# Layer 1 of a four-layer residual chain turned round: rows stationary, weights moving, activations transposed

## The chip, the core and the metric

The kernel runs on one core of a Trainium2 chip. The metric is the device time of one launch in microseconds (us). The engines are TensorE (PE; its weight loads are listed apart as PEld), VectorE (DVE), ScalarE (ACT), GpSimd (POOL) and SyncE (SP), each with a queue of its own that it works off in order. PSUM is where TensorE's results land; a bank holds 512 f32 per partition.

## What is computed

x has 64 batches of 32 rows of 512 values, 2048 rows in all. Four layers follow each other, each adding to x. Layer 1 is a gated MLP with three rank-16 adapters chosen per batch; it is what the change is about.

```python
def lora_add(base, inp, A, B):
    Ab = A[layer_idx][lora_indices]
    Bb = B[layer_idx][lora_indices]
    t = jnp.einsum('bri,bni->bnr', Ab, inp)
    return base + jnp.einsum('bor,bnr->bno', Bb, t) * SCALE        # SCALE 0.5, rank 16
gate = lora_add(jnp.einsum('bnh,fh->bnf', x, W_gate), x, A_gate, B_gate)   # h 512, f 1376
up = lora_add(jnp.einsum('bnh,fh->bnf', x, W_up), x, A_up, B_up)
act = jax.nn.silu(gate) * up
down = lora_add(jnp.einsum('bnf,hf->bnh', act, W_down), act, A_down, B_down)
...
x = x + _L0_cond_ref(x, ...)                       # layer 1, above
x = x + _L1_cond_ref(x, itok_B_0_15, ...)          # a 32x32 mix of the rows of each batch
x = x + _L2_cond_ref(x, itok_B_0_7, ...)           # 512x512 product, top-2 of 8 experts of rank 16
x = x + _L3_cond_ref(x, L3_cond_weights, itok_B_0_15)   # another 32x32 mix
```

All inputs are f32. Each f32 operand of a product is split into a high and a low part (type fp32r), and each product is three matmuls: high x high, high x low, low x high.

## The kernel before

**Layer 1, tiles.** The rows go in 8 groups (`g`) of 256, and F = 1376 in 11 chunks (`f`) of 128, the last of 96; a step `s` is one chunk of one group, 88 steps. In `gate_up_base` a chunk of W_gate or W_up is stationary (128 of H by 128 of F) and the transposed rows `xt` move, 256 columns: 2 weights x 4 pieces of H x 3 matmuls. So gate and up stand in PSUM with F on the partitions, which is what the down product needs as its stationary operand. `gate_up_adapters` adds the rank products: B of the chunk stationary, t moving, 2 x 3 matmuls of 256. `down` has 128 rows of the activations stationary and W_down moving: 2 row tiles x 2 halves of H x 3 matmuls of 288 columns, 256 of W_down and 32 of A_down beside them. `x_a` makes t = A x of the next group (24 matmuls of 256), and `transpose_td` and `down_adapters` finish the adapter of the down product, one step into the next group.

**Engines beside it.** ScalarE applies silu (L691) and makes every high part (L673, L677); VectorE multiplies by up (L867) and makes the low parts (L833, L891); GpSimd makes the low parts of W_down (L634) and issues the gathers of the adapters' tables (L572: `a`, `b`, `bd`). The order of all this is one list, `lane_jobs(s)`, that ScalarE, VectorE and (for W_down) GpSimd walk through alike; TensorE waits for `s_lo` with the number of a job in it. `plain_loads(s)` is the order of SyncE's loads, `gathers(s)` that of GpSimd's. PSUM holds three gate/up tiles, two down tiles and one for t and td.

**Weights.** W_gate, W_up and W_down are loaded and split once, during the first group, and stay in SBUF. SyncE's queue holds the loads back at two places: until the gathers of A have landed ("adapters first"), and until TensorE is within five chunks (`LOADS_AHEAD`).

**The end of layer 1.** In the last three steps the first tiles of layers 2 to 4 are mixed in (`l1`, `transpose_x2`, `l2_base`); the loop behind them takes 16 tiles of 128 rows through these layers.

## Time and profile before

| | us |
|---|---|
| median of 3 runs (lowest, highest) | 635.86 (635.08, 636.76) |
| the profiled execution | 636.53 |
| its span, first to last instruction | 634.6 |
| its mean granted TensorE clock | 0.992 |
| busy: PE, DVE, ACT, POOL | 604.6, 300.7, 202.4, 211.1 |
| layer 1, up to its last product | about 526 |

The profile is one execution. A matmul's duration is longer than its place in the stream, since matmuls are pipelined: what a matmul costs is read from the start times of its neighbours in the timeline. In the names, out<-in, buffer numbers are left out.

### The profile page before, as it was taken

What the parts mean: (1) busy time and instruction counts of PE and PEld (TensorE: products, weight loads), DVE (VectorE), ACT (ScalarE), POOL (GpSimd) and SP (SyncE); (2) the same over time, 40 slices, a digit from 0 to 9 for tenths busy, and PEclk for the clock granted to TensorE, in tenths of its full rate; (3) what the DMA queues carried; (4) which work ended last, traced back from release to release, by engine and by line L of the source; (5) the groups of instructions that cost most, each with busy time, mean ns of one, the idle gap of its engine ahead of it and who ended that gap; (6) DMA issues with size and microseconds to landing.
All of it is one profiled execution on the core that took longest, in us unless ns stands there. A gap on an engine that the chain in (4) does not pass through costs nothing.

```text
span 634.6 us, 11455 instructions
## 1 busy us (share of the span) xinstructions
PE 604.6 (95%) x4659; PEld 593.2 (93%) x4659; DVE 300.7 (47%) x748; ACT 202.4 (32%) x514; POOL 211.1 (33%) x230
## 2 busy tenths in 40 slices
PE   4797899999999999999999999999999998999996
PEld 4797899999999999999999999999999998888885
DVE  4575344234324332442333234333432257998997
ACT  4463332232223222322232223222323243333421
POOL 4347225111511241033113211420145714565541
PEclk9899799999999999999999999999999999999999
DMA  6875024102510241033104212411142112222212
GB/s 202 259 249 173 27 67 159 54 11 74 164 39 24 79 151 34 24 110 120 40 20 134 93 41 58 136 56 37 34 149 107 53 33 68 68 67 88 79 53 81
DMA packets 26612, 55.79 MB, mean 88 GB/s; under 512 B 4224, under 2 KB 7744, under 8 KB 26560
## 3 DMA queue, kind: packets, MB, share of 16 engines
q1 hardware_dynamic: 18608, 31.17, 15.0%
q0 software_dynamic: 7808, 23.86, 12.6%
q8 instruction: 36, 0.59, 0.4%
q14 instruction: 16, 0.13, 0.1%
q10 hardware_dynamic: 144, 0.03, 0.0%
HBM read 46.66 MB, written 8.39 MB: 87 GB/s over the span
## 4 chain that ended last, share of the span: by engine, by line
PE 83%; DVE 9%; issue 4%; DMA 1%; ACT 1%; POOL 1%; SPq 1%; POOLq 0%; DVEq 0%; ACTq 0%
PE gu_ps L1041 16%; PE gu_ps L1039 16%; PE gu_ps L1040 16%; PE down_ps L1039 8%; PE down_ps L1040 8%; PE down_ps L1041 8%; PE l_ps L1039 2%; PE l_ps L1041 2%; DVE route L940 2%; PE l_ps L1040 2%; DVE x L958 2%; DVE route L939 1%; PE tg_ps L1039 1%; PE tg_ps L1041 1%; PE tg_ps L1040 1%
## 5 line engine op out<-in xcount | busy, mean ns | idle before, releaser
L1039 PE MATMUL gu_ps<-xt,wgu_sb 128*128 128x256 f32 (+1 forms) x704 | 201.3, 286 | 8.3 <-DVE wgu_sb L891 8.3
L1041 PE MATMUL gu_ps<-xt,wgu_sb 128*128 128x256 f32 (+1 forms) x704 | 200.5, 285 | 0.4 <-issue 0.4
L1040 PE MATMUL gu_ps<-xt,wgu_sb 128*128 128x256 f32 (+1 forms) x704 | 200.5, 285 | 0.0
L1039 PEld LDWEIGHTS gu_ps<-xt,wgu_sb 128*128 128x128 f32 (+1 forms) x704 | 134.5, 191 | 8.4 <-DVE wgu_sb L891 8.3
L867 DVE TENSOR_TENSOR act<-act,gu_ps 128x256 f32<-128x256 f32 (+1 forms) x88 | 36.9, 420 | 217.9 <-ACT act L691 206.4
L1041 PEld LDWEIGHTS gu_ps<-xt,wgu_sb 128*128 128x128 f32 (+1 forms) x704 | 134.7, 191 | 0.7 <-issue 0.7
L1040 PEld LDWEIGHTS gu_ps<-xt,wgu_sb 128*128 128x128 f32 (+1 forms) x704 | 134.5, 191 | 0.0
L572 POOL DMA_INDIRECT b_sel_raw<-b_gu,idx_rank x48 | 46.4, 967 | 236.2 <-PE gu_ps L1041 222.3
L691 ACT ACTIVATE act<-gu_ps 128x256 f32<-128x256 f32 (+1 forms) x88 | 33.7, 383 | 261.4 <-PE gu_ps L1041 254.9
L1039 PE MATMUL down_ps<-wd_sb,act_hl 128*128 128x288 f32 (+1 forms) x352 | 104.9, 298 | 0.4 <-DVE act_hl L833 0.4
L1041 PE MATMUL down_ps<-wd_sb,act_hl 128*128 128x288 f32 (+1 forms) x352 | 104.0, 295 | 0.0
L1040 PE MATMUL down_ps<-wd_sb,act_hl 128*128 128x288 f32 (+1 forms) x352 | 103.9, 295 | 0.0
L572 POOL DMA_INDIRECT a_raw<-a_all,idx_batch x64 | 63.6, 993 | 69.9 <-DVE wd_sb L891 47.6
L1039 PEld LDWEIGHTS down_ps<-wd_sb,act_hl 128*128 128x128 f32 (+1 forms) x352 | 66.8, 190 | 0.7 <-DVE act_hl L833 0.7
L1040 PEld LDWEIGHTS down_ps<-wd_sb,act_hl 128*128 128x128 f32 (+1 forms) x352 | 66.6, 189 | 0.0
L1041 PEld LDWEIGHTS down_ps<-wd_sb,act_hl 128*128 128x128 f32 (+1 forms) x352 | 66.3, 188 | 0.0
L833 DVE TENSOR_TENSOR act_hl<-act,act_hl 128x256 fp32r<-128x256 f32 (+1 forms) x88 | 38.6, 439 | 38.3 <-ACT act_hl L673 33.1
L1039 PE MATMUL gu_ps<-t_hl,b_sel 128*128 128x256 f32 (+1 forms) x176 | 50.2, 285 | 1.8 <-DVE t_hl L833 1.8
L673 ACT CAST act_hl<-act 128x256 fp32r<-128x256 f32 (+1 forms) x88 | 35.8, 407 | 50.0 <-DVE act L867 45.8
L1041 PE MATMUL gu_ps<-t_hl,b_sel 128*128 128x256 f32 (+1 forms) x176 | 50.3, 286 | 0.0
L1040 PE MATMUL gu_ps<-t_hl,b_sel 128*128 128x256 f32 (+1 forms) x176 | 50.1, 285 | 0.0
L1039 PE MATMUL l_ps<-w2ra_hl,x2t_hl 128*128 128x328 f32 (+1 forms) x128 | 42.7, 334 | 0.6 <-DVE x_res L861 0.2
(132 smaller groups left out, 1017.8 us busy)
## 6 DMA issues: line engine op xcount, KB each, us to landing
wgu_sb_raw<-wgu SPq DMA_DIRECT2D x20, 256.0 KB, 5.7
xt_raw<-x_t SPq DMA_DIRECT2D x16, 256.0 KB, 3.1
x_res<-x_rows SPq DMA_DIRECT2D x8, 512.0 KB
x_after_l<-x_res SPq DMA_DIRECT2D x8, 512.0 KB
x<-x_after_l SPq DMA_DIRECT2D x16, 256.0 KB, 3.1
out<-y SPq DMA_DIRECT2D x15, 256.0 KB, 2.1
wd_sb_raw<-wd SPq DMA_DIRECT2D x10, 256.0 KB, 5.7
w_raw<-w2ra_t SPq DMA_DIRECT2D x1, 1296.0 KB
```

What stands on the lines that cost most here:

```text
L572: nc.gpsimd.indirect_dma_start(out=dst, out_offset=None, in_=table, in_offset=bass.IndirectOffsetOnAxis(ap=idx, axis=0)).then_inc(s, 16)
L673: sc.copy(out_, in_).then_inc(s_hi, 1)
L691: sc.activation(act[0:k, s % 2, :], gu_ps[s % GU_BANKS][0:k, 0, :], ACT.Silu).then_inc(s_silu, 1)
L833: ve.tensor_tensor(out_, raw, high.bitcast(F32), ALU.subtract).then_inc(s_lo, 1)
L867: ve.tensor_tensor(act[0:k, s % 2, :], act[0:k, s % 2, :], gu_ps[s % GU_BANKS][0:k, 1, :], ALU.mult).then_inc(s_mul, 1)
L939: link(ve.tensor_scalar(g1, const("iota"), ids[:, 1:2], w1, ALU.is_equal, ALU.mult))
L940: link(ve.tensor_tensor(g0, g0, g1, ALU.add))
L958: ve.tensor_tensor(halves(x3[:, t % 3, :], a, b), halves(x2[:, t % 3, :], a, b), base_of(t, a, b), ALU.add).then_inc(s_x3, 1)
L1039: pe.matmul(out_, stationary[0], moving[0], start=start, stop=False, skip_group_check=True)
L1040: pe.matmul(out_, stationary[0], moving[1], start=False, stop=False, skip_group_check=True)
L1041: return pe.matmul(out_, stationary[1], moving[0], start=False, stop=stop, skip_group_check=True)
```

## The change

- **Rows stationary.** The rows go in 16 tiles (`i`) of 128, F in three chunks (`n`) of 352, 512 and 512 columns, the narrow one first; 48 steps. `gate` and `up` have 128 rows of `xt` stationary and the weights moving, up to 512 columns. Each gate and each up has a PSUM bank of its own, two of each; down has one tile instead of two.
- **A x.** The columns of A (128) lie beside the narrow chunk's gate columns, so that t comes out of the same matmuls, 480 columns wide. Only the first tile has it apart (`x_a`).
- **Transposes.** The activations now have rows on the partitions. `transpose_act` turns the 128-column pieces of a chunk (3, 4 and 4) by a matmul against the identity; high and low part are made from its PSUM tile `act_t`. `transpose_t` turns t (2), `transpose_td` td (1).
- **Rank products stacked.** t is written twice side by side, so that its transpose holds it twice, in partitions 0 to 63 and 64 to 127: the upper copy as high part, the lower as low part. One matmul against B's high part does two of the three products, a second one on 64 rows the third (`stacked`). B is gathered doubled, 128 rows for four batches, for each tile of 128 rows.
- **Loads.** Weight pieces of a quarter chunk; SyncE's two hold-backs are gone. The loads of x, its stores and the residual go by tile.
- **Second stage.** The same instructions; layer 2's mix uses one PSUM tile, not four, and the hand-over at the end of layer 1 is ordered anew.

```diff
-GROUP = 256
-NG = ROWS // GROUP
...
+TR = TB * RANK
...
+CHUNKS = [(1024, F), (0, 512), (512, 1024)]
+NC = len(CHUNKS)
+STEPS = NT * NC
...
 def plain_loads(s):
...
-                + ["adapters first", ("wgu", GU_BANKS, 0), ("wgu", GU_BANKS, 1), ("wd", 0)]
...
+        return ([("x", 0, 0), first[0], first[1], ("x", 0, 1)] + first[2:] + wgu_items(0, 1)
+                + wgu_items(1, 0) + [("wd", f) for f in pieces_of(0)] + wgu_items(1, 1)
+                + wgu_items(2, 0) + [("wd", f) for f in pieces_of(1)] + wgu_items(2, 1)
+                + [("x", 1, 0)] + [("wd", f) for f in pieces_of(2)])
...
-        gu_ps = [ps(f"gu_ps{i}", [2, GROUP], banks_a) for i in range(GU_BANKS)]
-        down_ps = [ps(f"down_ps{i}", [2, H], banks_a) for i in range(TILES)]
-        tg_ps = ps("tg_ps", [2, GROUP], banks_a)
+        gu_ps = [[ps(f"gu_ps{i}_{m}", [H], banks_a) for m in range(2)] for i in range(2)]
+        down_ps = ps("down_ps", [2, H], banks_a)
+        act_t = ps("act_t", [HC, P], banks_a)
+        t_ps = ps("t_ps", [HC, P], banks_a)
...
+                elif kind == "act":
+                    s = job[1]
+                    sc.wait_ge(s_actt, s + 1)
                     if s >= 2:
                         sc.wait_ge(s_d, s - 1)
-                    hi(act_hl[0:k, s % 2, 0, :], act[0:k, s % 2, :])
+                    for k, j0, j1 in act_blocks(s):
+                        ins = sc.copy(act_hl[0:k, s % 2, 0, j0:j1, :], act_t[0:k, j0:j1, :])
+                    ins.then_inc(s_hi, 1)
...
+            def stacked(out_, stationary, moving):
+
+
+                pe.matmul(out_, stationary, moving[0], start=False, stop=False, skip_group_check=True)
+                return pe.matmul(out_, stationary[0:TR], moving[1][0:TR], start=False, stop=True,
+                                 skip_group_check=True)
...
+                    mm = product(out_, x_of(i, c), gate_moving(i, n, c), c == 0, False)
...
+                    product(up_of(s), x_of(i, c), wgu_parts(n, 1, c)[1:], c == 0, False)
...
+            def transpose_act(s):
+                pe.wait_ge(s_mul, s + 1)
+                if s >= 1:
+                    pe.wait_ge(s_lo, s_lo_of(("act", s - 1)))
+                for j, f in enumerate(pieces_of(s % NC)):
+                    w = cw(f)
+                    mm = pe.transpose(act_t[0:w, j, :], act[:, s % 2, j * P:j * P + w], ident)
+                mm.then_inc(s_actt, 1)
...
             for s in range(STEPS):
...
+                i, n = divmod(s, NC)
+                gate(s, 0, HC // 2)
+                if n == 1 and i >= 1:
+                    transpose_td(i - 1)
+                gate(s, HC // 2, HC)
+                if s >= 1:
+                    transpose_act(s - 1)
+                up(s, 0, HC // 2)
+                if n == 1 and i >= 1:
+                    down_adapters(i - 1)
+                if s == STEPS - 1:
+                    l1(0)
+                up(s, HC // 2, HC)
+                if n == 0:
+                    if i == 0:
+                        x_a(0)
+                    transpose_t(i)
+                else:
+                    adapters(s)
...
+                if s >= 1:
+                    down(s - 1)
...
+                if n == 0:
+                    adapters(s)
```

TensorE before, around the transposes of td (`tg_ps<-const_sb,td`) in the second chunk of a later group; `gu_ps` is the PSUM of gate and up, `xt` the rows, `wgu_sb` the weights:

```order
L1041 MATMUL gu_ps<-xt,wgu_sb 128x256
L1115 MATMUL tg_ps<-const_sb,td 128x128 [waits s_mask]
L1115 MATMUL tg_ps<-const_sb,td 128x128
L1039 MATMUL gu_ps<-xt,wgu_sb 128x256
L1040 MATMUL gu_ps<-xt,wgu_sb 128x256
...
L1039 MATMUL gu_ps<-t_hl,b_sel 128x256 [waits s_lo]
...
L1039 MATMUL down_ps<-wd_sb,act_hl 128x288 [waits s_mask,s_x1,s_lo]
```

TensorE after, in the narrow chunk of a later tile, from the last gate matmul to the rank products; `act_t` and `t_ps` are the PSUM tiles of the transposes, `wg_sb` and `wu_sb` the narrow chunk's weights:

```order
L1055 MATMUL gu_ps_0<-wg_sb,xt 128x480
L1120 MATMUL act_t<-const_sb,act 128x128 [waits s_lo,s_mul]
L1120 MATMUL act_t<-const_sb,act 128x128 x3
L1053 MATMUL gu_ps_1<-wu_sb,xt 128x352
...
L1100 MATMUL t_ps<-const_sb,t_m 128x128 [waits s_tm]
L1100 MATMUL t_ps<-const_sb,t_m 128x128
L1053 MATMUL down_ps<-wd_sb,act_hl 128x288 [waits s_lo]
...
L1060 MATMUL gu_ps_0<-b_sel,t_hl 128x352 [waits s_lo]
L1061 MATMUL gu_ps_0<-b_sel,t_hl 128x352
```

Stationary and moving operand have changed sides, the transposes stand between gate and up, and the down product behind them waits for the low part made from `act_t`.

ScalarE before, in the weight load of the first group, from A to the first silu (`agu_t` and `wd_sb<-a_raw` are A, `b_sel` is B):

```order
L677 CAST agu_t<-a_raw 128x512 [waits s_a_in]
L677 CAST agu_t_up<-a_raw 128x512 [waits s_a_in]
L677 CAST wd_sb<-a_raw 128x4x32 x4
L673 CAST b_sel<-b_sel_raw 128x512 [waits s_b_in0]
L673 CAST wgu_sb<-wgu_sb_raw 128x512 [waits s_wgu_in3_0]
L673 CAST t_hl<-t_raw 128x512 [waits s_mask]
L673 CAST b_sel<-b_sel_raw 128x512 [waits s_b_in1]
L673 CAST wgu_sb<-wgu_sb_raw 128x512 [waits s_wgu_in3_1]
L673 CAST wd_sb<-wd_sb_raw 128x2x256 [waits s_wd_in0]
L691 ACTIVATE act<-gu_ps 128x256 [waits s_gu]
```

ScalarE after, the same stretch of the first tile:

```order
L679 CAST wg_sb<-a_raw 128x4x128 [waits s_a_in]
L675 CAST b_sel<-b_sel_raw 128x704 [waits s_b_in0]
L675 CAST t_hl<-t_ps 128x256 [waits s_tt]
L675 CAST w_sb<-w_sb_raw 128x512 [waits s_wgu_in1_0_0]
L675 CAST w_sb<-w_sb_raw 128x512 [waits s_wgu_in1_0_1]
L675 CAST w_sb<-w_sb_raw 128x512 [waits s_wgu_in1_0_2]
L675 CAST w_sb<-w_sb_raw 128x512 [waits s_wgu_in1_0_3]
L691 ACTIVATE act<-gu_ps_0 128x352 [waits s_gu]
```

The high part of t now stands right behind B's, ahead of all wide weight pieces (`w_sb`); before, six weight pieces of 512 stood ahead of A, and two more between A and the first silu. VectorE's low parts follow in the same order.

## Rows read from the trace of the kernel before

**Rows 1.** The page, part 1: busy us of the engines, share of the span, instructions.

```profile
PE 604.6 (95%) x4659; PEld 593.2 (93%) x4659; DVE 300.7 (47%) x748; ACT 202.4 (32%) x514; POOL 211.1 (33%) x230
```

**Rows 2.** Busy time by stage: stretch and its length, engines' busy us, granted clock, DMA.

```profile
8.34:93.69 85.35, 74.86 (x552) 74.08 (x553) 47.71 (x92) 39.04 (x96) 37.68 (x35) 0.94 0.51 161
93.69:500.00 406.31, 406.31 (x3301) 406.31 (x3300) 145.14 (x341) 115.44 (x307) 110.02 (x115) 1.00 0.25 78
500.00:526.40 26.40, 25.65 (x192) 24.51 (x190) 12.89 (x31) 10.32 (x22) 8.26 (x12) 1.00 0.11 30
526.40:634.60 108.20, 97.78 (x619) 88.34 (x618) 93.00 (x283) 34.17 (x86) 52.99 (x65) 1.00 0.22 74
```

**Rows 3.** Timeline of PE in group 2: start us, us, engine, line, op.

```profile
199.90 0.28 PE L1039 MATMUL gu_ps<-xt,wgu_sb 128*128 128x256 f32 x1
...
201.94 0.28 PE L1041 MATMUL gu_ps<-t_hl,b_sel 128*128 128x256 f32 x1
202.06 0.30 PE L1039 MATMUL down_ps<-wd_sb,act_hl 128*128 128x288 f32 x1
...
203.65 0.28 PE L1039 MATMUL tg_ps<-xt,agu_t 128*128 128x256 f32 x1
```

**Rows 4.** Timeline of PE: td transposes of group 1, and those of group 2.

```profile
155.26 0.38 PE L1115 MATMUL tg_ps<-const_sb,td 128*128 128x128 f32 x2
155.40 0.36 PE L1039 MATMUL gu_ps<-xt,wgu_sb 128*128 128x256 f32 x1
155.60 0.28 PE L1040 MATMUL gu_ps<-xt,wgu_sb 128*128 128x256 f32 x1
...
216.83 0.38 PE L1115 MATMUL tg_ps<-const_sb,td 128*128 128x128 f32 x2
```

**Rows 5.** Timeline of PE in the second stage: widths of 328, 320 and 512, four transposes.

```profile
540.65 0.31 PE L1039 MATMUL l_ps<-w2ra_hl,x2t_hl 128*128 128x328 f32 x1
...
542.32 0.31 PE L1041 MATMUL l_ps<-w2ra_hl,x2t_hl 128*128 128x328 f32 x1
...
544.30 0.60 PE L1147 MATMUL x2t_ps<-const_sb,x 128*128 128x128 f32 x4
544.65 0.39 PE L1039 MATMUL l_ps<-w2ra_hl,x2t_hl 128*128 128x320 f32 x1
544.88 0.31 PE L1040 MATMUL l_ps<-w2ra_hl,x2t_hl 128*128 128x320 f32 x1
...
545.62 0.28 PE L1039 MATMUL l_ps<-b_hl,hgt_hl 128*128 128x256 f32 x1
...
546.32 0.39 PE L1039 MATMUL l_ps<-x_hl,bd_hl 128*128 128x512 f32 x1
...
547.72 0.31 PE L1039 MATMUL l_ps<-w2ra_hl,x2t_hl 128*128 128x328 f32 x1
```

**Rows 6.** Timeline: a transpose to PSUM, then its low part on DVE.

```profile
512.83 0.60 PE L1147 MATMUL x2t_ps<-const_sb,x 128*128 128x128 f32 x4
...
514.28 0.68 DVE L902 TENSOR_TENSOR x2t_hl<-x2t_ps,x2t_hl 128x512 fp32r<-128x512 f32 x1
```

**Rows 7.** Waits of PE before 93.6 us: us in total, times, longest.

```profile
PE gu_ps L1039 <- DVE wgu_sb L891: 8.3, 1, 8.3
PE tg_ps L1039 <- DVE agu_t L891: 6.6, 1, 6.6
PE gu_ps L1039 <- DVE t_hl L833: 1.8, 1, 1.8
```

**Rows 8.** Groups of instructions, shapes apart: busy us, mean ns, idle time before.

```profile
L891 DVE TENSOR_TENSOR wgu_sb<-wgu_sb_raw,wgu_sb 128x512 fp32r<-128x512 f32 x20 | 16.7, 861 | 4.4 <-ACT wgu_sb L673 4.4
...
L634 POOL TENSOR_TENSOR wd_sb<-wd_sb_raw,wd_sb 128x512 fp32r<-128x512 f32 x10 | 13.1, 1307 | 24.5 <-ACT wd_sb L673 24.4
...
L673 ACT CAST wgu_sb<-wgu_sb_raw 128x512 fp32r<-128x512 f32 x20 | 11.8, 617 | 2.3 <-DMA wgu_sb_raw<-wgu 2.0
```

**Rows 9.** Busy time in the densest stretch of the weight load.

```profile
32.00:40.00 8.00, 7.56 (x61) 7.32 (x60) 5.99 (x10) 5.01 (x11) 3.92 (x3) 1.00 0.96 318
```

More of the change, by code:

```diff
@@ L78, with cw, width, pieces_of @@
 L2_COLS = sum(L2_WIDTH)
-def w13_tiles(n):
-    return range(n * NT // W13_STEPS, (n + 1) * NT // W13_STEPS)
-def cw(c):
-    return P if c < FC - 1 else LASTW
+def cw(f):
+    return min(P, F - f * P)
+def width(n):
+    return CHUNKS[n][1] - CHUNKS[n][0]
+def pieces_of(n):
+    return range(CHUNKS[n][0] // P, -(-CHUNKS[n][1] // P))
+WD_ORDER = [f for n in range(NC) for f in pieces_of(n)]
 CONST_COLS = {}
@@ L146, in gathers @@
[L146 to L155 removed]
+    if s >= 1 and s + 1 < STEPS:
+        out.append(("b", s + 1))
+    if n < 2 and i + 1 < NT:
+        out += [("a", i + 1, b) for b in range(n * TB // 2, (n + 1) * TB // 2)]
+    if n == 2:
+        out.append(("bd", i))
+    if 0 <= s - W13_FIRST < NT:
+        out.append(("w13", s - W13_FIRST))
+    return out
@@ L626, in _ @@
             for s in range(-1, STEPS):
-                first = [it for it in gathers(s) if it[0] == "b" or s < 0]
+                first = [it for it in gathers(s) if s < 0 or it[0] == "b"]
                 for it in first:
@@ L894, in add_x2 @@
+                ins.then_inc(s_lo, 1)
             def add_x2(t):
@@ L1129, in mix, with down_adapters @@
+            def down_adapters(i):
+                pe.wait_ge(s_lo, max(s_lo_of(("td", i)), s_lo_of(("bd", i))))
+                for half in range(2):
+                    cols = slice(half * HALF, (half + 1) * HALF)
+                    mm = stacked(base_cols(i)[:, half, :], td_hl[:], [bd_hl[:, part, cols] for part in range(2)])
+                mm.then_inc(s_dl, 1)
             def mix(bank, t, m, x_hl):
@@ L1256, with act_blocks @@
 N_IDX = IDX_RANK + 3 + 2
-def first_step(k):
-    return k // PAIRS * FC + k % PAIRS * 2
-def mask_no(job):
-    order = [j for s in range(-1, STEPS + FC) for j in lane_jobs(s) if j[0] in ("t", "td")]
-    return order.index(job) + 1
+CHUNKS_AT = [sum(width(k) for k in range(n)) for n in range(NC)]
+def act_blocks(s):
+    ks = [cw(f) for f in pieces_of(s % NC)]
+    full = sum(k == P for k in ks)
+    return [(P, 0, full)] + [(k, full, full + 1) for k in ks[full:]]
 def kernel(**inputs):
```

871 lines of the change are left out of this document (408 added, 463 removed).

## The prediction, made before the changed kernel was run

> **What bounds the kernel now.** The page's first part gives TensorE 95% of the span [rows 1]; that share alone doesn't say that matmuls set the end, so the second view is the busy time by stage [rows 2]. There the reader sees four stretches. From 8.34 to 93.69 us the weights arrive and TensorE runs 552 matmuls in 85.35 us. From 93.69 to 500 us TensorE is busy for all of 406.31 us, at a granted clock of 1.00, while VectorE works 145 us and ScalarE 115 us. From 500 to 526.4 us the second stage's first tiles are mixed in. From 526.4 us on layers 2 to 4 run, 108.2 us, with VectorE busy 93.0. So layer 1 is bound by the column stream of TensorE and the tail mostly by VectorE. The third view is the timeline, for the price of a matmul: not its duration (0.28 us, pipelined), but the distance from start to start.
>
> **Prices, start to start.** 256 columns: from 199.90 to 201.94 are 17 steps, 0.120 us each; 288 columns: 12 steps from 202.06 to 203.65, 0.1325 us [rows 3]. 328 columns: 11 steps from 540.65 to 542.32, 0.1518; 320 columns: 5 steps from 544.88 to 545.62, 0.148; 512 columns: 6 steps from 546.32 to 547.72, 0.2333 [rows 5]. At full clock a column is 0.4167 ns, so the rest of one matmul is 13.3 ns at 256 columns and 20 ns at 512: wider is hardly cheaper by the column. 352 and 480 columns don't occur; a line between 328 and 512 gives 0.1624 and 0.2191. Four transposes in a row take 0.35 us and make the first matmul behind them 0.23 instead of 0.148, together 0.43 [rows 5]; two take 0.14 and 0.08 behind them, 0.22 [rows 4]. Three are then 0.36 and one is 0.16.
>
> **The change, layer 1 in the steady part.** A group of 256 rows takes 216.83 - 155.26 = 61.57 us [rows 4]. The sum gives the same: 366 matmuls of 256 columns (264 gate and up, 66 rank, 24 for A x, 12 of the last rank product) x 0.120 = 43.9, 132 of 288 x 0.1325 = 17.5, two transposes 0.2; 61.6. Of the changed kernel, one tile of 128 rows is:
> gate and up of the two wide chunks with their stacked rank products, 2 x (12 + 12 + 4) = 56 of 512 columns, 13.07 us;
> gate of the narrow chunk with A x attached, 12 of 480, 2.63;
> its up and rank products, 12 + 4 of 352, 2.60;
> down, unchanged, 66 of 288, 8.75;
> the last rank product, 4 of 256, 0.48;
> 11 transposes of the activations in blocks of 4, 4 and 3, two of t and one of td, 0.43 + 0.43 + 0.36 + 0.22 + 0.16 = 1.60.
> Together 29.13 us, 58.26 for 256 rows: 3.31 less than 61.57. Times 8 it is **26.5 us less**. What goes: a third of the rank products (the low part of t now sits in the idle 64 rows of the stationary), half of the columns of A x, and the 32 padded columns of F. What comes: 14 transposes per tile where there was one.
>
> **Does it still run without a wait?** Before, no wait of TensorE is found between 93.69 and 500 us [rows 2]. The new chain is: silu, product, transposes, high part, low part, then down. The tightest place is at the narrow chunk, where down of the last wide chunk follows the transposes after only 12 up matmuls and the transposes of t: 0.43 + 12 x 0.1624 + 0.22 = 2.6 us from the first transpose. What has to fit in: a chain of the same shape and size stands in the trace, four transposes starting at 512.83 and the low part ending at 514.28 + 0.68 = 514.96, so 2.13 us [rows 6], with VectorE's mask of t beside it and done before. Slack 0.5 us. The other chunks have 12 x 0.2333 + 4 x 0.2333 = 3.7 us for it. I take no wait, and keep 0.5 us per tile, 8 us, as the upper bound. VectorE has 145 busy in 406 us and ScalarE 115 [rows 2]; the wider operations carry the same elements, plus b gathered and split for each 128 rows instead of 256, some 2.5 us per tile and engine: room enough. The doubled gathers of b (11 MB more) lie beside 78 GB/s of traffic where 318 are reached [rows 2, 9], with a whole chunk, some 10 us, to land in.
>
> **The start.** Before: the 552 matmuls up to 93.69 us are 420 of 256 and 132 of 288 columns, 50.4 + 17.5 = 67.9 us of stream in 85.35, so 17.4 us are lost after the first matmul, besides the 8.3 in front. The waits show where: 6.6 for A of the next group, 1.8 for t [rows 7]; the rest is the lower clock (0.94 over the stretch [rows 2]) and short waits. After: the same weights must be in place within one tile, 29 us, not within 61. The first pieces are smaller (a quarter of a chunk, half of the rows), so the first matmul comes about 0.9 us earlier, at 7.4. The narrow chunk's 24 matmuls end near 13.5, a part of them at the low clock. Then A x, mask, transposes, high, low and the gathered rank weights stand in one row in front of the first rank product, with nothing for TensorE beside them: about 6 us, to 19.5. From there VectorE must split 16 wide weight pieces at 0.861 [rows 8], 13.8 us, two rank tables of twice the width (0.68 for 512 [rows 6], so 1.3 each), 2.6, and some 2.5 of activations; 19 us. ScalarE has 16 + 7 pieces x 0.617 [rows 8] plus 4.5, also 19, and the transfers, about 10 MB at 318 GB/s [rows 9], end near 35 us. So the last rank product of tile 0 ends near 39.5, with down of its last two chunks still to come. By stream alone that point would be 7.4 + 21.8 = 29.2. Lost: 10.3, and 1.7 more for the clock after the pause, 12; bounds 8 (pieces at 0.7) and 16 (a gather behind the now unthrottled weight queue). **Gain at the start: 17.4 - 12 + 0.9 = 6.3 us** (2 to 10).
>
> **The end of layer 1.** The pieces of the second stage that are mixed in are the same. One PSUM tile for layer 2 instead of four makes each product wait for the sum before it; I find these sums done in time, but the residual sum of the last tile now stands right in front of the next matmul, about 0.8 us. From there on nothing is changed: 108.2 us.
>
> **Sum.** -26.5 - 6.3 + 0.8 = -32.0 us. The profiled execution had a span of 634.6 and a time of 636.5, 0.7 over the median of 635.9; I carry the difference over to the median: 635.9 - 32.0 = **603.9 us**.
>
> **A rule of the Trainium skill against it.** The four transposes above are 128x128 in f32, and cost 0.43 us together. The Trainium skill, "TensorE: Matmul & The Clock Gate", Part 4, gives some 275 ns for one transpose within a kernel. By the page's price 14 of them would be 3.85 us per tile, 36 us more in all. The trace has that figure only as the duration of one, not as its place in the stream. [...]
>
> **Rivals.** (a) *Wide matmuls at the narrow overhead*: the 20 ns at 512 columns belong to those products, which read other tiles, and gate and up pay 13.3 as at 256. Then 56 x 6.6 ns + 28 x about 4 ns = 0.48 us per tile less, 7.7 in all: 596. For it: no gate product of that width is in the trace. Against: 320 and 328 columns already lie above the line of 256 and 288. (b) *A wait per chunk or tile*, the chain of transposes late at down: 0.5 to 1 us per tile, 8 to 16: 612 to 620. For it: 0.5 us of slack, and two engines in order with gathers in front. Against: the chain in the trace fits. (c) *Transposes that don't pipeline with their neighbours*, each at its full duration (0.38 for two [rows 4], so 0.27 for one): 14 x 0.27 = 3.8 instead of 1.6 per tile, +35 us, **639, slower**. It tips above 1.60 + 32 / 16 = 3.6 us of transposes per tile. Against: four in 0.35 [rows 5], in the same form. (d) *The start doesn't improve*, the weights being needed twice as fast: 610.
>
> **Chances.** Forecast (with the start anywhere in its bounds) 0.62, its own range 599 to 610; (a) 0.14; (b) 0.15; (c) 0.03; something else that adds a wait in each chunk 0.03; (d) counted beyond the bounds 0.03. Range 595 to 616: it takes in (a) and the lower half of (b). A difference below 0.3%, 1.9 us, can't be told from none. Faster by more 0.94, within 0.02, slower 0.04.
>
> **What would show it.** In the timeline after: 0.233 us from start to start in gate and up of 512 columns, 0.162 and 0.219 at 352 and 480; 0.43 per block of four transposes with the next matmul; a period of 29.1 us from one td transpose to the next; no wait of TensorE between the second and the fifteenth tile. The first td transpose shows the start. Wrong if the period is above 30, if TensorE waits at down's first matmul for the low part, or if its clock falls below 1.00 in the steady part.

## The result, and the profile after

| | us |
|---|---|
| before, median of 4 (lowest, highest) | 635.80 (635.08, 636.76) |
| forecast | 603.9 (595 to 616) |
| after, median of 4 (lowest, highest) | 658.89 (657.33, 662.34) |
| ratio after to before, 95% interval | 1.037 (1.032 to 1.042) |
| span of the profiled executions, before and after | 634.6 and 659.0 |

The change makes the kernel 3.7% slower, where 5% faster was forecast. The miss is 55 us. The page of after, part 1, against [rows 1]:

```profile
PE 626.0 (95%) x3359; PEld 517.3 (78%) x3359; DVE 324.0 (49%) x686; ACT 205.1 (31%) x413; POOL 234.8 (36%) x238
```

TensorE has 1300 instructions fewer and is busy 21 us longer. Its busy time by stage (stretch and length, busy us of PE, PEld, DVE, ACT and POOL, granted clock, DMA share, GB/s), against [rows 2]:

```profile
0.00:66.10 66.10, 48.34 (x211) 38.74 (x212) 38.54 (x64) 32.39 (x62) 36.76 (x32) 0.87 0.63 209
66.10:497.00 430.90, 430.90 (x2259) 349.43 (x2258) 165.19 (x296) 119.43 (x230) 130.58 (x124) 1.00 0.31 100
497.00:545.00 48.00, 47.47 (x269) 39.64 (x268) 23.85 (x44) 16.90 (x33) 14.16 (x17) 1.00 0.28 94
545.00:659.00 114.00, 99.27 (x626) 89.47 (x625) 96.44 (x283) 36.34 (x90) 53.34 (x65) 1.00 0.20 68
```

From 66.1 to 497 us TensorE is busy for all of 430.9 us at a granted clock of 1.00. So no wait and no clock explains the loss: the stream itself is longer than the sum said. Its period from one td transpose to the next, which is one tile of rows, follows from the first and the fifteenth of them in the timeline of PE, (513.81 - 66.25) / 14 = **31.97 us**; forecast 29.1:

```profile
66.25 0.27 PE L1144 MATMUL t_ps<-const_sb,td 128*128 128x128 f32 x1
...
513.81 0.27 PE L1144 MATMUL t_ps<-const_sb,td 128*128 128x128 f32 x1
```

Within the period the same timeline shows which distance is wrong. First the places with an answer as forecast: 480 columns, 352 columns and the transposes (start us, duration us, engine, line, operation; what counts is the distance of the starts):

```profile
278.84 0.38 PE L1053 MATMUL gu_ps<-wg_sb,xt 128*128 128x480 f32 x1
...
281.24 0.38 PE L1055 MATMUL gu_ps<-wg_sb,xt 128*128 128x480 f32 x1
281.46 0.60 PE L1120 MATMUL act_t<-const_sb,act 128*128 128x128 f32 x4
281.81 0.41 PE L1053 MATMUL gu_ps<-wu_sb,xt 128*128 128x352 f32 x1
282.06 0.33 PE L1054 MATMUL gu_ps<-wu_sb,xt 128*128 128x352 f32 x1
...
283.65 0.32 PE L1055 MATMUL gu_ps<-wu_sb,xt 128*128 128x352 f32 x1
```

480 columns take 2.40 / 11 = 0.218 us each, 352 take 1.59 / 10 = 0.159, and the block of four transposes 0.35 + 0.25 - 0.16 = 0.44. Then the rank products of a wide chunk:

```profile
305.72 0.39 PE L1055 MATMUL gu_ps<-w_sb,xt 128*128 128x512 f32 x1
305.95 0.39 PE L1060 MATMUL gu_ps<-b_sel,t_hl 128*128 128x512 f32 x1
306.26 0.50 PE L1061 MATMUL gu_ps<-b_sel,t_hl 64*128 64x512 f32 x1
306.69 0.49 PE L1060 MATMUL gu_ps<-b_sel,t_hl 128*128 128x512 f32 x1
307.12 0.50 PE L1061 MATMUL gu_ps<-b_sel,t_hl 64*128 64x512 f32 x1
307.55 0.40 PE L1053 MATMUL down_ps<-wd_sb,act_hl 128*128 128x288 f32 x1
307.78 0.30 PE L1054 MATMUL down_ps<-wd_sb,act_hl 128*128 128x288 f32 x1
```

Up to 305.95 the starts are 0.23 us apart (the first two lines, and those ahead of them). Then they are 0.31, 0.43, 0.43, 0.43 and 0.23 apart, and the last of these was to be 0.13. The only thing that sets L1061 apart is the form: its stationary has 64 rows, 64*128 in the place of 128*128. The weight loads of the same place tell how the distance arises; in brackets is the idle time ahead of a load and what it was put down to ("issue": nothing that the profile shows):

```profile
305.72 0.19 PEld L1060 LDWEIGHTS gu_ps<-b_sel,t_hl 128*128 128x128 f32 x1
306.26 0.18 PEld L1061 LDWEIGHTS gu_ps<-b_sel,t_hl 64*128 64x128 f32 x1 [0.35 <-issue]
306.69 0.19 PEld L1060 LDWEIGHTS gu_ps<-b_sel,t_hl 128*128 128x128 f32 x1 [0.24 <-issue]
307.12 0.18 PEld L1061 LDWEIGHTS gu_ps<-b_sel,t_hl 64*128 64x128 f32 x1 [0.24 <-issue]
307.55 0.19 PEld L1053 LDWEIGHTS down_ps<-wd_sb,act_hl 128*128 128x128 f32 x1 [0.25 <-issue]
307.65 0.19 PEld L1054 LDWEIGHTS down_ps<-wd_sb,act_hl 128*128 128x128 f32 x1
```

Normally a load starts with the matmul ahead of its own (the load of L1060 at 305.72, its matmul at 305.95). At each change between 128 and 64 rows, at 306.26, 306.69, 307.12 and 307.55, the load starts only with its own matmul, and the stream is longer by about the 0.19 us that a load takes. That these changes cost the time was the theory to be tested.

Two smaller differences are left, the start and the second stage. The start: the waits of PE before 90 us (us in total, times, longest), against [rows 7], and the granted clock between 16 and 30 us:

```profile
PE gu_ps L1053 <- DVE wg_sb L837: 11.1, 2, 6.5
PE t_ps L1100 <- DVE t_m L846: 3.5, 2, 2.0
...
```

```profile
16.00:22.00 6.00, 3.11 (x14) 2.92 (x14) 1.98 (x4) 1.34 (x2) 0.00 (x0) 0.50 1.04 373
22.00:30.00 8.00, 6.99 (x20) 4.54 (x19) 4.79 (x8) 6.60 (x14) 3.10 (x3) 0.60 1.07 372
```

Then the second stage, whose code is nearly the same: from the first to the last hgt transpose (the transpose of `hg`, layer 2's gated rank values, one per tile) it takes 97.7 us before (529.1 to 626.9) and 101.1 after (549.7 to 650.9). Its period per tile of rows is either 6.5 to 6.7 or 7.1 to 7.2 us, but for the last one of 3.5; before, 4 of 15 periods are long, after 9 of 15. In a short one VectorE (first three lines) and GpSimd (fourth) look so, in the timeline of before:

```profile
561.03 0.29 DVE L939 TENSOR_SCALAR route<-const_sb,route 128x8 f32<-128x8 f32 x1
561.35 1.14 DVE L940 TENSOR_TENSOR route<-route 128x8 f32<-128x8 f32 x1
562.53 0.29 DVE L944 TENSOR_TENSOR hg<-l_ps,route 128x128 f32<-128x128 f32 x1
...
561.12 1.34 POOL L623 TENSOR_TENSOR x_hl<-x,x_hl 128x512 fp32r<-128x512 f32 x1 [2.57 <-ACT x_hl L742]
```

In a long one, in the timeline of after (the same instructions stand 12 lines lower in the kernel, on GpSimd 11):

```profile
603.40 1.43 DVE L951 TENSOR_SCALAR route<-const_sb,route 128x8 f32<-128x8 f32 x1
604.86 0.65 DVE L952 TENSOR_TENSOR route<-route 128x8 f32<-128x8 f32 x1
605.54 0.29 DVE L956 TENSOR_TENSOR hg<-l_ps,route 128x128 f32<-128x128 f32 x1
...
603.50 1.30 POOL L634 TENSOR_TENSOR x_hl<-x,x_hl 128x512 fp32r<-128x512 f32 x1 [2.58 <-ACT x_hl L743]
```

A routing operation on 8 values takes 0.16 to 0.29 us when undisturbed, and 1.14 or 1.43 when GpSimd's subtraction of 512 columns runs at the same time. In the first case one operation is held, in the second two in a row: from the start of L939 to that of L944 1.50 us pass, from L951 to L956 2.14. That is 0.64 us for one tile, the difference between the periods. When GpSimd's subtraction starts doesn't tell the two apart, as far as the traces resolve it: behind the start of L951 it is 0.095 us in the long tile at 589.59 us and in the short one at 596.82 alike, and it is 0.09 to 0.10 in all tiles of both kernels where the two meet but the first two of each, which have 0.04 and are long. What decides between them is not shown.

### The profile page after: what moved, and what is told of

It reads as the page before. It is cut to its first block, busy times and chain, and to the rows that moved or that the text cites. A ratio compares the mean times of both kernels' runs of the same rounds, so it can differ in the third digit from the quotient of the medians.

```text
span 659.0 us, 8713 instructions
## 1 busy us (share of the span) xinstructions
PE 626.0 (95%) x3359; PEld 517.3 (78%) x3359; DVE 324.0 (49%) x686; ACT 205.1 (31%) x413; POOL 234.8 (36%) x238
## 4 chain that ended last, share of the span: by engine, by line
PE 81%; DVE 9%; POOL 3%; DMA 2%; ACT 2%; issue 2%; SPq 0%; POOLq 0%; DVEq 0%; ACTq 0%
PE gu_ps L1053 12%; PE gu_ps L1055 11%; PE gu_ps L1054 11%; PE down_ps L1053 8%; PE down_ps L1054 7%; PE down_ps L1055 7%; PE gu_ps L1061 6%; PE gu_ps L1060 4%; PE act_t L1120 3%; PE l_ps L1053 2%; PE l_ps L1055 2%; PE l_ps L1054 2%; DVE route L951 2%; PE down_ps L1061 2%; DVE x L970 1%
## 5 line engine op out<-in xcount | busy, mean ns | idle before, releaser
L1053 PE MATMUL gu_ps<-w_sb,xt 128*128 128x512 f32 x256 | 108.3, 423 | 1.9 <-DVE w_sb L837 1.9
L1055 PE MATMUL down_ps<-wd_sb,act_hl 128*128 128x288 f32 (+1 forms) x352 | 104.3, 296 | 0.0
L1055 PE MATMUL gu_ps<-w_sb,xt 128*128 128x512 f32 x256 | 101.3, 396 | 0.0
L1054 PE MATMUL gu_ps<-w_sb,xt 128*128 128x512 f32 x256 | 100.6, 393 | 0.0
L576 POOL DMA_INDIRECT a_raw<-a_all,idx_batch x64 | 75.6, 1181 | 48.1 <-DVE wd_sb L837 28.6
L885 DVE TENSOR_TENSOR act<-act,gu_ps 128x512 f32<-128x512 f32 (+1 forms) x48 | 30.3, 631 | 101.8 <-ACT act L691 101.8
L691 ACT ACTIVATE act<-gu_ps 128x512 f32<-128x512 f32 (+1 forms) x48 | 26.6, 553 | 170.8 <-PE gu_ps L1061 170.8
L698 ACT CAST act_hl<-act_t 128x256 fp32r<-128x256 f32 (+1 forms) x64 | 27.3, 452 | 149.7 <-PE act_t L1120 145.3
L837 DVE TENSOR_TENSOR act_hl<-act_t,act_hl 128x256 fp32r<-128x256 f32 (+1 forms) x64 | 32.0, 520 | 76.5 <-ACT act_hl L698 75.5
L837 DVE TENSOR_TENSOR b_sel<-b_sel_raw,b_sel 64x1024 fp32r<-64x1024 f32 (+1 forms) x48 | 54.1, 1128 | 14.9 <-ACT b_sel L675 14.9
L1053 PEld LDWEIGHTS gu_ps<-w_sb,xt 128*128 128x128 f32 x256 | 48.5, 189 | 15.6 <-issue 2.8
L1055 PEld LDWEIGHTS gu_ps<-w_sb,xt 128*128 128x128 f32 x256 | 48.3, 189 | 11.0
L1054 PEld LDWEIGHTS gu_ps<-w_sb,xt 128*128 128x128 f32 x256 | 48.6, 190 | 7.1
L675 ACT CAST b_sel<-b_sel_raw 128x1024 fp32r<-128x1024 f32 (+1 forms) x48 | 45.6, 951 | 3.0 <-DMA b_sel_raw<-b_gu,idx_rank 3.0
L1061 PE MATMUL gu_ps<-b_sel,t_hl 64*128 64x512 f32 (+1 forms) x96 | 46.0, 479 | 0.0
## 6 DMA issues: line engine op xcount, KB each, us to landing
w_sb_raw<-wgu SPq DMA_DIRECT2D x16, 256.0 KB, 10.3
wd_sb_raw<-wd SPq DMA_DIRECT2D x10, 256.0 KB, 10.3
```

The source lines that it names most:

```text
L576: nc.gpsimd.indirect_dma_start(out=dst, out_offset=None, in_=table, in_offset=bass.IndirectOffsetOnAxis(ap=idx, axis=0)).then_inc(s, 16)
L675: sc.copy(out_, in_).then_inc(s_hi, 1)
L691: sc.activation(act[:, s % 2, 0:width(s % NC)], gate_of(s), ACT.Silu).then_inc(s_silu, 1)
L698: ins = sc.copy(act_hl[0:k, s % 2, 0, j0:j1, :], act_t[0:k, j0:j1, :])
L837: return ve.tensor_tensor(out_, raw, high.bitcast(F32), ALU.subtract)
L885: ve.tensor_tensor(a, a, up_of(s), ALU.mult).then_inc(s_mul, 1)
```

## Experiments

The kernel before was run in each job; it had 638.85 us in the first (the first four kernels below), 636.06 in the second (the next four) and 633.97 in the third (the last three). Ratios are against it.

### 1. All 128 rows

The kernel after, with the second matmul of `stacked` on all rows, and the low part of B written for all rows. The lower half of t in the stationary is its low part, so this adds the product low x low.

```diff
-                    ins = lo(l[0:TR], raw[0:TR], h[0:TR])
+                    ins = lo(l, raw, h)
...
-                return pe.matmul(out_, stationary[0:TR], moving[1][0:TR], start=False, stop=True,
+                return pe.matmul(out_, stationary, moving[1], start=False, stop=True,
...
```

> The changed kernel, with the second matmul of each stacked rank product on all 128 rows of the stationary operand instead of 64 (the low part of B is made for all 128 rows, at the same number of elements per partition). Theory: the steady period of 31.97 us per tile is 2.84 above the forecast because a matmul on a 64-row stationary between matmuls on 128 rows can't have its weights loaded ahead, and neither can the next one. Then the four rank matmuls of a wide chunk take 0.93 us instead of 1.70, the period falls to about 29.0 us, and the time by some 47 us to 612 (608 to 616). Rival: the cost comes from going between the gate bank and the up bank, or from the width; then the period stays at 32 and the time at 659.

Measured: 611.99 (611.13 to 614.16), ratio 0.958 (0.955 to 0.961). Number and width of the matmuls are the same as after, there is more arithmetic in them, and the time is 47 us less, or 50 if each of the two is taken against the kernel before of its own job (26.9 below it here, 23.1 above it there). The timeline of PE at a wide chunk's rank products:

```profile
279.67 0.39 PE L1060 MATMUL gu_ps<-b_sel,t_hl 128*128 128x512 f32 x1
279.90 0.39 PE L1061 MATMUL gu_ps<-b_sel,t_hl 128*128 128x512 f32 x1
...
280.71 0.29 PE L1054 MATMUL down_ps<-wd_sb,act_hl 128*128 128x288 f32 x1
```

From the first rank matmul to the second matmul of down it is 1.04 us, in the kernel after 1.83: 0.79 per chunk. The period is (466.93 - 63.65) / 14 = 28.81 us, 3.16 less than after; times 16 that is 50.6 us. The theory holds, and with full rows the steady part is even 0.3 us per tile shorter than the forecast's 29.13.

### 2. The 64-row matmuls side by side

The kernel after, with the order 128, 128, 64, 64 in each group in the place of 128, 64, 128, 64. There are as many matmuls of 64 rows as after, and half as many changes. The last rank product (`down_adapters`) is ordered in the same way.

```diff
-                for m in range(2):
-                    mm = stacked((gate_of, up_of)[m](s), t_hl[:, m, :],
-                                  [b_sel[:, s % 2, part, m * w:(m + 1) * w] for part in range(2)])
+                for part in range(2):
+                    for m in range(2):
+                        mm = half_stacked(part, (gate_of, up_of)[m](s), t_hl[:, m, :],
+                                          b_sel[:, s % 2, part, m * w:(m + 1) * w])
...
```

> The changed kernel with the order of the four rank matmuls turned: both 128-row ones first (gate, up), then both 64-row ones; the same in the last rank product. If the cost sits at each change between 128 and 64 rows, two of four changes go, 0.45 us of each group of four, 4 groups per tile: 29 us less, 630. If it sits at each 64-row weight load, wherever it stands, only the loads back to 128 rows in between are saved, one of four changes: 13 us less, 645. If the row count has nothing to do with it: 659.

Measured: 632.8 in one run, and a period of (490.39 - 65.13) / 14 = 30.38 us, between 28.81 (no change of rows) and 31.97 (four changes per group). Half the changes cost half: 1.57 of 3.16 us. So what is paid is the change, not the matmul of 64 rows. The weight loads say the same:

```profile
323.77 0.29 PEld L1066 LDWEIGHTS gu_ps<-b_sel,t_hl 64*128 64x128 f32 x2 [0.35 <-issue]
324.43 0.19 PEld L1053 LDWEIGHTS down_ps<-wd_sb,act_hl 128*128 128x128 f32 x1 [0.36 <-issue]
```

The first line holds two 64-row loads, 0.29 us together, where one takes 0.18: the second one starts ahead of its own matmul again (that one stands at 324.11). Idle time stands ahead of the first 64-row load and of the first 128-row one, and nowhere between.

A change costs 3.16 / 16 = 0.20 us, 16 of them being in a tile of the kernel after. In the lines of the kernel after this has two parts: the first 64-row matmul comes 0.08 us later than 0.23 behind its neighbour, before its load has begun, and the matmul behind the last change 0.10 us later than its width asks for, with the load in between. So the price is the size of one load, but not simply the load's own time; what the first part is, no run here separates.

### 3. Weights held back

The kernel of experiment 1, with SyncE's hold-back of before put back in: the wide weights' loads wait until A has landed.

```diff
-                + wgu_items(1, 0) + [("wd", f) for f in pieces_of(0)] + wgu_items(1, 1)
+                + ["adapters first"] + wgu_items(1, 0) + [("wd", f) for f in pieces_of(0)] + wgu_items(1, 1)
```

> e1_full_rows, and SyncE's queue waits again for the gathers of A before it issues the wide weight pieces, as the kernel before did. In the changed kernel A landed at 15.9 us and the rank table at 19.5, behind 8 MB of queued weights, and TensorE idled 4.6 us in front of A x at a falling clock. Theory: the gathers land 2 to 4 us earlier and the first td transpose comes 2 to 4 us earlier than in e1_full_rows, time 2 to 4 us less. Rival: the wide pieces then come late by as much, and the time is the same within 1 us or longer.

Measured: 606.96 (605.54 to 609.77), ratio 0.952 (0.948 to 0.956). Only a part of the 5 us against experiment 1 is the start: the first td transpose comes at 62.23 us, 1.4 earlier. One execution of each is thin evidence for that size: the kernels without the hold-back and with full or 96 rows have it at 63.65, 63.53 and 66.31 (experiments 1, 4 and 5), those with it at 62.23 and 60.97 (3 and 8, the same code up to there). The rest is the second stage, 96.5 us from the first to the last hgt transpose in the place of 102.6, which this edit doesn't touch. In the start, the wait of TensorE before A x went from 9.4 to 7.3 us (with the first matmul's), and the waits behind it rose: for the masked t from 4.5 to 5.8, for wide weights from 4.2 to 5.1.

### 4. Routing ahead of the sum

The kernel of experiment 1, with VectorE's routing operations ahead of the sum for x3, so that they are through before GpSimd's subtraction starts.

```diff
+                if 1 <= i < NT - 1:
+                    route_gates(i)
...
-                if 1 <= i < NT - 1:
-                    route_gates(i)
```

> e1_full_rows, and in the second stage VectorE computes the routing gates of a tile ahead of the sum x3 of the tile before, not behind it. Theory: the second stage took 112 us after and 108 before only because the short routing operations of VectorE (0.16 to 0.29 us) stand still for the whole of GpSimd's 1.3 us subtraction of x3 when that starts a hair before them: ten of 16 are hit at the costly place in one trace and four in the other, at a start that differs by 0.01 us. With the gates first they don't meet that subtraction, all routing operations stay under 0.5 us, and the period per tile is at most 6.6 us in each tile: second stage 100 to 106 us, time 3 to 8 us under e1_full_rows. Rival: the sum x3, 1.6 us later, becomes the late one for the matmuls, and the period stays or grows.

Measured: 617.19 (615.18 to 617.86), ratio 0.967 (0.964 to 0.970): 5 us slower than experiment 1 by the medians. In the profiled executions the second stage takes 104.3 us in the place of 102.6, and every period but the last is long. No routing operation of this group is held any more (L951 takes 0.28 us in each tile but the first), but now x3 comes later, and TensorE stands still once per tile in front of layer 2's product: in one tile that product starts at 549.46 us, VectorE's sum for x3 ends at 549.36. The waits of PE in the second stage:

```profile
PE l_ps L1053 <- issue: 11.8, 14, 1.3
```

In experiment 1 TensorE waited 9.2 us there for the hg behind the held operation. So the hold is gone at the place where it was looked for, and the new order costs a little more than it. Beside it another operation is held now: L939, the difference of the two best scores, takes 0.85 us in most tiles and 678 ns on average, after 189.

### 5. 96 rows

The kernel of experiment 1 with the second matmul on 96 rows (`stationary[0:96]`, `moving[1][0:96]`); it leaves out half of the low x low that experiment 1 adds.

> The kernel after with the second matmul of each stacked rank product on 96 of the 128 rows (the padding rows 64 to 95 hold zeros on one side). Theory A, the price comes from a stationary that fills only half of the rows (64): 96 rows behave like 128, the weight loads stay one matmul ahead, a wide chunk's rank products take 0.93 us, the period from td transpose to td transpose is 28.75 us, and the time 610 to 615 us. Theory B, any stationary with fewer rows than its neighbours breaks the stream: 1.70 us, period 32.0, time about 659 us. For A: down's own 96-row stationaries stand between 128-row ones at 0.13 us each in both traces.

Measured: 611.06 in one run, period (470.56 - 66.31) / 14 = 28.88 us. The timeline of PE:

```profile
282.87 0.39 PE L1060 MATMUL gu_ps<-b_sel,t_hl 128*128 128x512 f32 x1
283.09 0.40 PE L1061 MATMUL gu_ps<-b_sel,t_hl 96*128 96x512 f32 x1
283.32 0.40 PE L1060 MATMUL gu_ps<-b_sel,t_hl 128*128 128x512 f32 x1
```

96 rows between 128 cost nothing. So a smaller stationary as such is not what is paid for.

### 6. 64 rows in the kernel before

The kernel before, with the third matmul of each rank product of gate and up on 64 of its 128 rows.

```diff
+                    mm = pe.matmul(out_, b_sel[0:64, k, 1, cols], t_hl[0:64, g % 2, 0, m, :], start=False,
+                                   stop=m == 1, skip_group_check=True)
```

> The kernel before, with one edit: the third of the three matmuls of each rank product in gate and up reads 64 of the 128 rows of its stationary and of its moving tile. It leaves out the other 64 rows' part of that term. Columns, number of matmuls and everything else stay. Theory: each change of TensorE between 128 and 64 rows costs about 0.2 us more than a matmul of the same width, wherever it stands. 176 such matmuls with a change before and one behind each, some of them masked by their width: 0.25 to 0.35 us each, 44 to 62 us, so 680 to 698 us. Rival: the price belongs to the new layout (512 columns in one bank, other buffers), not to the rows: then the time stays at 636 to 639 us.

Measured: 705.68 in one run, 69.6 us more than before in the same job (69.2 by the spans). The theory's sign holds and its size doesn't: 680 to 698 was expected. The timeline of PE:

```profile
200.59 0.28 PE L1085 MATMUL gu_ps<-t_hl,b_sel 128*128 128x256 f32 x1
200.71 0.28 PE L1087 MATMUL gu_ps<-t_hl,b_sel 128*128 128x256 f32 x1
200.92 0.38 PE L1089 MATMUL gu_ps<-t_hl,b_sel 64*128 64x256 f32 x1
201.23 0.39 PE L1085 MATMUL gu_ps<-t_hl,b_sel 128*128 128x256 f32 x1
201.45 0.28 PE L1087 MATMUL gu_ps<-t_hl,b_sel 128*128 128x256 f32 x1
```

Where every distance was 0.12 us, it is now 0.21, 0.31 and 0.22: the price begins one matmul ahead of the 64-row one and ends one behind it. The period of a group goes from 61.57 to 243.52 - 173.71 = 69.81 us, 8.24 for 22 such matmuls, **0.375 us for each**. 176 of them make 66 us. The first group, with the weight load in it, is 1.9 us longer beyond that, and the second stage 1.8 (99.5 for 97.7). Nothing of the changed kernel's layout is in this run, so the price belongs to the rows. At 256 columns it is 0.375 per matmul, with a change on either side; at 512 columns 0.79 for two.

### 7. Mask first

The kernel of experiment 3, with VectorE's mask of the first tile's t ahead of the split of B.

```diff
-        return ... + wgu_items(0, 1) + [("at", 0), ("b", 0)]
+        return ... + wgu_items(0, 1) + [("at", 0), ("tm", 0), ("b", 0)]
```

> All 128 rows in the second rank matmul, the wide weights' transfers held until the A table has landed, and in addition VectorE masks tile 0's t before it splits tile 0's gathered b, not behind it. Theory: of the 4.4 us that TensorE waited for t_m in the kernel with the first two edits, 2 to 4 go, the first td transpose comes at 59 to 60 us instead of 62.2, and the time is 2 to 3 us under it: about 604. Rival: the split of b is late next, or the weight splits (5.1 us of waits on w_sb), and take it back: the first td transpose at 62 and the time 606 to 608.

Measured: 605.68 (604.91 to 608.12), ratio 0.951 (0.948 to 0.954). The first td transpose comes at 61.5 us, 0.7 earlier than in experiment 3, but experiment 8, with experiment 3's order in this place, has it at 60.97, and experiment 10, with this one, at 61.23: a gain is not shown. In the waits the rival of the expectation is seen. The longest wait for the masked t went from 4.4 to 3.2 us, and the high and low part of t, now behind B's split, are waited for 3.3 us instead of 1.0.

### 8. GpSimd's subtraction in pieces

The kernel of experiment 3, with the subtraction for the low part of x3 in four pieces.

```diff
-                pool.tensor_tensor(x3_hl[:, t % 2, 1, :], x3[:, t % 3, :],
-                                   x3_hl[:, t % 2, 0, :].bitcast(F32), ALU.subtract).then_inc(s_x3lo, 1)
+                for a in range(0, H, P):
+                    ins = pool.tensor_tensor(x3_hl[:, t % 2, 1, a:a + P], x3[:, t % 3, a:a + P],
+                                             x3_hl[:, t % 2, 0, a:a + P].bitcast(F32), ALU.subtract)
+                ins.then_inc(s_x3lo, 1)
```

> All 128 rows in the second rank matmul, the wide weights' transfers held until the A table has landed, and GpSimd's subtraction for the low part of x3 (512 columns, 1.3 us) cut into four of 128 columns. Theory: a short VectorE routing operation that starts just behind GpSimd's subtraction is held until it ends, so with pieces it is held 0.4 us at most, never 1.4; the second stage from the first to the last hgt transpose takes 96 to 97 us whatever the phase, and the time is 604 to 607. Rival: four starts cost GpSimd more than they free, x3's low part comes later and TensorE waits for it: stage 98 to 104 us, time 608 to 614.

Measured: **598.67** (598.09 to 599.30), ratio 0.940 (0.937 to 0.944), better than expected. The pieces cost GpSimd 1.77 us in the place of 1.3, and the routing operations that were held are nearly as short as undisturbed ones (284 and 166 ns); those of after (first line) and of this kernel (the two others), by line (busy us, mean ns of one):

```profile
L951 DVE TENSOR_SCALAR route<-const_sb,route 128x8 f32<-128x8 f32 x16 | 16.0, 999 | 0.0
```

```profile
L956 DVE TENSOR_SCALAR route<-const_sb,route 128x8 f32<-128x8 f32 x16 | 5.8, 364 | 0.0
L957 DVE TENSOR_TENSOR route<-route 128x8 f32<-128x8 f32 x16 | 5.0, 310 | 0.6
```

The period is 6.21 to 6.22 us ten times in a row, from 516.77 to 578.91, the stage takes 90.0 us in the place of 96.5, and TensorE waits 0.6 us in all of it. Another operation is held: L944, the difference of the two best scores, takes 813 ns on average, beside GpSimd's subtraction for x1. Busy time from 529.2 to 579 us:

```profile
529.20:579.00 49.80, 49.80 (x332) 47.61 (x329) 47.30 (x145) 19.21 (x46) 34.78 (x63) 1.00 0.25 80
```

### 9. Pieces in the kernel before

The same edit in the kernel before.

> The kernel before, with one edit: GpSimd's subtraction for the low part of x3 (512 columns) is cut into four of 128 columns. Theory: the hold between GpSimd and VectorE in the second stage has nothing to do with layer 1. The stage from the first to the last hgt transpose, 97.7 us before, comes to 90 to 92 us as it did in the turned kernel with pieces (90.0), and the time is 628 to 631 us. Rival: the gain of pieces needs the new order of the second stage's items: the stage stays at 96 to 98 and the time at 634 to 637.

Measured: 628.33 (627.62 to 628.75), ratio 0.991 (0.989 to 0.994), 5.6 us by the medians. The stage takes 617.05 - 526.93 = 90.1 us, in the place of 97.7: the hold has nothing to do with the turned layer 1. It was in the profile of before, as a cost of 7.6 us that I took for the stage's own work.

### 10. Pieces for x1 too

The kernel of experiment 8, with the order of experiment 7 and with GpSimd's subtraction for the low part of x1 in four pieces as well.

> The version with 128 rows, held weights and pieces (598.7), and two more edits: VectorE masks t of tile 0 before it splits b, and GpSimd's subtraction for the low part of x1 (512 columns, 1.28 us) is cut into four as well. With pieces for x3 alone the op held was another one, VectorE's difference of the two best scores, 1.07 us in the place of 0.16, at the same time as that subtraction. Theory: this hold goes too, 0.5 to 0.9 us per tile: period 5.4 to 5.8 us instead of 6.21, stage from the first to the last hgt 79 to 84 us, time 588 to 593. Rival: something else bounds the period at 6.2 (TensorE's own matmuls of the stage, or GpSimd with 8 starts more): stage 89 to 91, time 597 to 599.

Measured: 598.64 (598.14 to 599.40), ratio 0.944 (0.942 to 0.947). The operation that experiment 8 left held (L944 there, L946 here) did go, from a mean of 813 ns to 264, and nothing is gained: stage 90.0 us, period 6.21. The rival is right: behind experiment 8 the stage is bound by TensorE (busy for 49.80 of 49.80 us), and VectorE's hold lies beside it.

### 11. 32 rows

The kernel of experiment 1 with the second matmul on 32 rows; it leaves out half of the product of t's high part with B's low part.

> The second matmul of each stacked rank product on 32 of the 128 rows; it leaves out half of the low part of that product. At 96 rows the price did not appear (28.9 us per tile), at 64 it did (32.0). Theory A, a stationary of at most half of the rows costs: 32 rows cost like 64, period 32.0, time 657 to 662. Theory B, exactly 64 rows cost, 32 and 96 don't: period 28.8, time 608 to 615.

Measured: 657.54 in one run, period (513.47 - 66.19) / 14 = 31.95 us, as with 64 rows. The loads of L1061 here (first line) and in experiment 5 (second line; its matmul starts at 283.09):

```profile
306.07 0.18 PEld L1061 LDWEIGHTS gu_ps<-b_sel,t_hl 32*128 32x128 f32 x1 [0.35 <-issue]
282.87 0.19 PEld L1061 LDWEIGHTS gu_ps<-b_sel,t_hl 96*128 96x128 f32 x1
```

So 32 and 64 rows pay, 96 and 128 don't. This fits what the Trainium skill, "TensorEngine Tiling (Array Packing)", says in "Tiling Modes": the array has configurations of 128, 64 and 32 rows per tile, and "Changing tiling mode (not just tile) drains the TensorE". The runs agree with it in all five cases (128, 96, 64, 32, and 64 grouped), if 96 rows count as the configuration of 128; nothing but the missing price shows that here.

## Why the prediction was wrong

The sum, term by term. Measured are the profiled executions; the start is the time by which the first td transpose is later than the stream in front of it.

| term | forecast | measured |
|---|---|---|
| layer 1, steady: 16 periods less 8 x 61.57 | -26.5 | 16 x 31.97 - 492.6 = +18.9 |
| start | -6.3 | 27.5 - 25.8 = +1.7 |
| end of layer 1 | +0.8 | +0.7 |
| second stage | 0 | +3.4 |
| sum (span: 659.0 - 634.6 = +24.4) | -32.0 | +24.7 |

**The step that failed** is the term "gate and up of the two wide chunks with their stacked rank products, 2 x (12 + 12 + 4) = 56 of 512 columns, 13.07 us", and with it "its up and rank products, 12 + 4 of 352, 2.60" and "the last rank product, 4 of 256, 0.48". They count the second matmul of each stacked pair at the price of a 128-row one. It is `stationary[0:TR]` in the diff, 64 rows, a form that layer 1 of the kernel before doesn't have, and the prediction set neither a bound nor a rival for it, because only width was taken for a form. Its sign of being wrong, a period above 30 us, is what came. Per tile there are four groups of two: three in gate and up, one at the last rank product. Experiment 1 measures the term: 3.16 us per tile, 50.6 in all. Without it the time is 611.99 us, inside the range and 8 above the forecast. That it lies inside is in part luck: in the profiled execution the second stage was 4.9 us longer and the start lost 2.2 where it was to gain 6.3, and the steady part, 5.1 shorter than the sum, took some of it back.

**What else was sized.** Everything else in the steady part came out 0.32 us per tile shorter than the sum (28.81 for 29.13): 0.159 for 0.162 at 352 columns, 0.218 for 0.219 at 480, 0.230 for 0.233 at 512, but four transposes 0.44 for 0.43. So the trace agrees with what the prediction drew from [rows 3] to [rows 5] and not with the 275 ns for one transpose that it quoted beside them from the Trainium skill, "TensorE: Matmul & The Clock Gate", Part 4: rival (c), the only slower one, named the right sign and the wrong place. Rival (a) did not come for gate and up (0.231 us apart at 512 columns for the most part, where it asked for 0.227; only the rank products had that), nor (b): from 66.1 to 497 us TensorE has no wait. The chain of transposes, high and low part fits, as [rows 6] said.

**The start** was to lose 12 us behind the first matmul, after 7.4 in front: 19.4. The first matmul came at 6.54. Up to the td transpose at 66.25 the stream holds 40 matmuls of 352, 12 of 480, 58 of 512, 12 of 128 (0.11 us apart at full clock in experiment 3) and 66 of 288 columns, 8 of 64 rows, 15 transposes and four groups' price of 0.79, by the distances above 38.8 us. So 27.5 are lost, 20.9 of them behind the first matmul. 11.2 are waits: 4.6 before A x, 3.5 for the masked t, 1.9, 1.0 and 0.2. Some 10 are the clock and short gaps, where 1.7 were set down: TensorE stood still for 4.6 us before 17.4, the granted clock was 0.50 from 16 to 22 us (that is the 1.2 GHz level) and 0.60 from 22 to 30. Before, it was 1.00 and 0.82 there. The first wait is a matter of the loads' order: wide weights ran ahead of A (a piece took 10.3 us from issue to landing, before 5.7). Experiment 3's hold-back brings A x from 16.24 to 13.44 us (13.2 to 13.9 in all four kernels with it) and the first td transpose 1.4 us earlier; experiment 7 only shifts the waits. The clock makes such single numbers uncertain: in experiment 5, which has no other edit in the start than experiment 1, it was 0.66 between 40 and 50 us, where experiment 1 had 1.00, and the transpose came 2.7 us later. How much of the rest is the clock alone was not measured.

**The second stage** was "unchanged: 108.2 us". Its instructions are, and its time isn't, since its period takes one of two values with the same code. With the same second stage the first to the last hgt transpose took 101.1 us (after), 102.6 (experiment 1), 96.5 (2, 3 and 5), 98.4 (7), 99.5 (6), 97.8 (11) and 97.7 (before). It should have had a range of its own, -1 to +5 us. Experiments 8 and 9 take the hold of these operations away and get 90.0 and 90.1. Which periods are long differs between these kernels; whether the edits elsewhere do that or each execution by itself, one profile of each can't tell.

**The end of layer 1** came as forecast: TensorE waits 0.94 us for the residual sum (547.82), before 0.23.

The best version run, experiment 8, is 6.0% faster than the kernel before and 9% faster than the change as it was made. It is the change with full rows in the rank products, the hold-back of the loads kept, and one subtraction of the second stage in pieces. Its span is 659.0 - 596.9 = 62.1 us shorter than that of after. The first td transpose comes 5.3 us earlier (3.2 of them the price of the four groups ahead of it), from the first to the sixteenth it takes 46.2 us less, all of it the rows, and the second stage takes 11.2 less; 0.5 is lost behind it.

## What to carry to other kernels

When a matmul is added, price it by its whole form, stationary rows included; if the trace has no such form beside its neighbours, give it a bound of one weight load (here 0.2 us) on each side at which the form changes. Filling a half-used stationary to full rows with data that may be added is cheaper here than using 64 or 32 rows among 128; if the rows can't be filled, stand such matmuls side by side. A stage "with nothing changed" whose period takes two values is to be given the width of both, and an operation on 8 values that takes 1 us in it is worth an experiment by itself.

## What the hardware showed

- **Rows of a stationary.** At a change between 128 and 64 (or 32) rows the weight load, 0.19 us, didn't run ahead of its matmul, and each change cost 0.20 us; between two 64-row matmuls it ran ahead again (experiment 2). Two 64-row matmuls between 128-row ones cost 0.79 us at 512 columns, one at 256 columns 0.375. 96 rows among 128 cost nothing.
- **VectorE and GpSimd.** While GpSimd subtracts 512 columns (1.3 us), some short VectorE operations are held, up to 1.43 us: the sum and the difference of two operands in SBUF on 8 values or 1 (L952 and L939), and the comparison L951, which reads a constant and two more values per partition from SBUF. Others are not: L956 of after, which reads PSUM and SBUF, kept its 0.29 us in the nine tiles in which it ran inside such a subtraction (291 ns on average over 16), and MAX8 (L938 in experiment 4), which has one operand in SBUF, its 0.17. Four pieces of 128 columns take 1.77 us together and hold the operations behind their start little (364 and 310 ns on average). The Trainium skill, "GPSIMD Engine Reference", section "Specifications", says that GpSimd shares its SBUF interfaces with VectorE, with contention for instructions that have two SBUF inputs or run in a 2-port mode; the trace agrees for the difference and the sum of two SBUF operands.
- **f32 transposes in a stream.** Four of 128x128 take 0.35 us and lengthen the next matmul's place by 0.09, after as in [rows 5].
